# The router's products of a four-layer kernel turned round: weights still, tokens streaming

## The reference

```python
x = x + _L0_ffn_ref(_layernorm(x, axis=-1), expert_sel, keys, values, route_scale)

def _L0_ffn_ref(x, expert_sel, keys, values, route_scale):
    sel_logits = jnp.einsum('btd,ed->bte', x, expert_sel)       # 16 experts, D = 256
    sel_probs = jax.nn.sigmoid(sel_logits)
    _, sel_index = jax.lax.top_k(sel_probs, 4)
    sel_val = jnp.take_along_axis(sel_probs, sel_index, axis=-1)
    sel_val = sel_val / jnp.clip(sel_val.sum(-1, keepdims=True), 1e-09) * route_scale
    ...
```

## Time and profile before

| | |
|---|---|
| median of 3 runs | 1512.51 us (1511.04 to 1518.49) |
| the profiled execution | 1518.33 us |
| its span, first to last instruction | 1516.5 us |
| mean granted TensorE clock | 0.906 |
| PE busy | 1309.8 us, 86% |
| PE weight loads busy | 800.3 us, 53% |
| DVE busy | 935.9 us, 62% |
| ACT busy | 455.5 us, 30% |
| POOL busy | 325.8 us, 21% |

### The profile page before, as it was taken

The page is one execution under the profiler, slowest core; times in us unless marked ns, Lnnn a source line. Parts: engine busy times, 40 slices in busy tenths (PEclk is TensorE's granted clock), DMA queues, the critical chain, the costliest instruction groups (busy, mean ns, idle before and its releaser), DMA issues. The chain is left out here.

```text
span 1516.5 us, 17699 instructions
## 1 busy us (share of the span) xinstructions
PE 1309.8 (86%) x5358; PEld 800.3 (53%) x5358; DVE 935.9 (62%) x3450; ACT 455.5 (30%) x821; POOL 325.8 (21%) x600
## 2 busy tenths in 40 slices
PE   2676968999999899989989999999797606999997
PEld 2354645556465455646546564564354504766674
DVE  6657788677777567767766776677975282121110
ACT  2433441142224215222431530422322333223211
POOL 3211220023012203301220320221203203333222
PEclk9967978999999799889999999999998757999999
DMA  9002001200300300030030003012000151344321
GB/s 286 8 1 71 17 1 28 43 18 15 85 17 1 99 1 17 15 85 17 1 99 17 1 24 76 16 23 64 0 1 1 58 202 44 88 119 129 84 25 18
DMA packets 44857, 72.56 MB, mean 48 GB/s; under 512 B 8085, under 2 KB 26648, under 8 KB 44634
## 3 DMA queue, kind: packets, MB, share of 16 engines
q1 hardware_dynamic: 38618, 62.90, 14.2%
q0 software_dynamic: 6144, 8.52, 3.2%
HBM read 58.31 MB, written 13.11 MB: 47 GB/s over the span
## 5 line engine op out<-in xcount | busy, mean ns | idle before, releaser
L714 POOL TENSOR_SCALAR ve<-mv 128x2 f32<-128x2 f32 x74 | 16.8, 227 | 607.8 <-DVE mv L972 607.7
L1484 PE MATMUL ps<-x,keys 128*128 128x512 f32 x256 | 133.0, 646 | 0.4 <-DVE hT L1064 0.4
L1638 PE MATMUL ps<-hT,values 128*128 128x512 f32 x256 | 118.6, 592 | 0.0
L2099 PE MATMUL experts_ps<-experts_yT,experts_fc 128*128 128x512 f32 x256 | 114.2, 605 | 1.3 <-ACT experts_yT L2022 1.3
L2111 PE MATMUL experts_ps<-experts_fc,experts_hT 128*128 128x256 f32 x512 | 112.1, 380 | 0.8 <-ACT experts_hT L2034 0.8
L1484 PE MATMUL ps<-zT_second,w 128*128 128x512 f32 x224 | 103.3, 602 | 7.0 <-ACT big L1446 6.3
L2111 PEld LDWEIGHTS experts_ps<-experts_fc,experts_hT 128*128 128x128 f32 x512 | 96.6, 190 | 14.7 <-ACT experts_hT L2034 1.6
L1484 PE MATMUL ps<-w,big 128*128 128x256 f32 x448 | 101.1, 385 | 1.6 <-ACT big L1446 1.6
L1997 DVE SCALAR_TENSOR_TENSOR experts_o<-experts_ps,experts_wh,experts_b2w 128x256 f32<-128x256 f32 x32 | 15.5, 484 | 140.2 <-PE experts_ps L2111 140.2
L1484 PEld LDWEIGHTS ps<-w,big 128*128 128x128 f32 x448 | 85.6, 193 | 15.4 <-ACT big L1446 4.0
L2034 ACT ACTIVATE experts_hT<-experts_ps,experts_b 128x512 f32<-128x512 f32 x64 | 44.0, 687 | 158.0 <-PE experts_ps L2099 158.0
(11 more groups left out here) (436 smaller groups left out, 2520.1 us busy)
## 6 DMA issues: line engine op xcount, KB each, us to landing
gT<-expert_gates SPq DMA_DIRECT2D x16, 1024.0 KB, 10.2
experts_fc<-in_fc1T SPq DMA_DIRECT2D x8, 1024.0 KB
experts_fc<-in_fc2T SPq DMA_DIRECT2D x8, 1024.0 KB
xT<-in_xT SPq DMA_DIRECT2D x8, 512.0 KB, 3.7
x<-in_x SPq DMA_DIRECT2D x8, 512.0 KB, 3.5
expert_table<-tb SPq DMA_DIRECT2D x7, 528.0 KB, 10.3
out_x<-x SPq DMA_DIRECT2D x7, 512.0 KB, 9.6
w<-in_W SPq DMA_DIRECT2D x2, 1024.0 KB, 8.4
```

The costliest lines, as they stand in the source:

```text
L714: nc.gpsimd.tensor_scalar(o, i, c, None, ALU.add).then_inc(*tick(*event))
L1484: last = nc.tensor.matmul(o, l, r_, start=start, stop=stop)
L1638: last = nc.tensor.matmul(bank("O2", k), S["values"][:, c, k * P:(k + 1) * P], hT[:, c % RING, :], start=(c == 0), stop=(c == HC - 1))
L2099: last = nc.tensor.matmul(g_bank(m), fc1[e % 3][:, k, m * P:(m + 1) * P], yT[e % 2][:, k, :], start=(k == 0), stop=(k == DC - 1))
```

## The change

The products are turned round. In `route` the 17 columns of `sel` stand still and the 512 tokens of `xp` stream past, for both `k`; the logits come out with experts on the partitions, in partitions 64 to 80 of bank LG. The one column of 1/256 stands still while `sq` streams past, into partition 96. A new step, `turn_route`, follows `route` in all three tables: ACT copies 33 partitions by 512 of LG to `lists`, and PE turns them back in four pieces of 33 by 128 into bank LT, from which DVE goes on as before, with 33 columns for each group of tokens instead of 18 (mean in column 16, mean of squares in 32). `lists` grows to 128 partitions.

```diff
-    (ATTEND, 0, "attend_out"), (ATTEND, 0, "route"), (MID, 0, "mlp", 0), (ATTEND, 0, "attend_sum"), (KERN, 0, "powers", 2),
+    (ATTEND, 0, "attend_out"), (ATTEND, 0, "route"), (ATTEND, 0, "turn_route"), (MID, 0, "mlp", 0), (ATTEND, 0, "attend_sum"), (KERN, 0, "powers", 2),
...
-    first += [(("OT", k), k) for k in range(DC)] + [(("LG",), 2), (("GT",), 3)]
+    first += [(("OT", k), k) for k in range(DC)] + [(("LG",), 2), (("LT",), 3), (("GT",), 2)]
...
-        lists = sb("lists", [32 + E0, T])
+        lists = sb("lists", [P, T])
         g16 = lists[32:32 + E0, :]
+        route_rows = slice(64, 64 + 33)
...
-                    lg = bank("LG")[:, 0:NT * (E0 + 2)].rearrange("p (t e) -> p t e", t=NT)
-                    v.wait_ge(*at(b, "filled", "LG"))
-                    nc.vector.tensor_copy(ms[:], lg[:, :, E0:E0 + 2]).then_inc(*tick("ms"))
+                    lg = bank("LT")[:, 0:NT * 33].rearrange("p (t e) -> p t e", t=NT)
+                    v.wait_ge(*at(b, "filled", "LT"))
+                    nc.vector.tensor_copy(ms[:], lg[:, :, E0:2 * E0 + 1:E0]).then_inc(*tick("ms"))
...
+            def turn_route(b):
+                evacuate(b, lists[route_rows, :], bank("LG")[route_rows, :], "LG")
...
                 pe.wait_ge(*at(b, "emptied", "OT", DC - 1))
-                parts = [p for t in range(NT) for p in contract(o[:, t * (E0 + 2):t * (E0 + 2) + E0 + 1], [
-                    (xp[:, k, t * P:(t + 1) * P], S["sel"][:, k, :]) for k in range(DC)])]
                 pe.wait_ge(*open_(b, "LG"))
-                for o_, l, r_, start, stop in parts:
-                    nc.tensor.matmul(o_, l, r_, start=start, stop=stop)
+                for k in range(DC):
+                    nc.tensor.matmul(o[64:64 + E0 + 1, :], S["sel"][:, k, :], xp[:, k, :], start=(k == 0), stop=(k == DC - 1))
                 pe.wait_ge(*at(b, "sq", DC - 1))
+                for k in range(DC):
+                    last = nc.tensor.matmul(o[96:97, :], S["sel"][:, k, E0:E0 + 1], sq[:, k, :], start=(k == 0), stop=(k == DC - 1))
+                last.then_inc(*tick("filled", "LG"))
+
+            def turn_route(b):
+                pe.wait_ge(*at(b, "emptied", "LG"))
+                pe.wait_ge(*open_(b, "LT"))
                 for t in range(NT):
-                    for k in range(DC):
-                        last = nc.tensor.matmul(o[:, t * (E0 + 2) + E0 + 1:(t + 1) * (E0 + 2)], sq[:, k, t * P:(t + 1) * P],
-                                                S["sel"][:, k, E0:E0 + 1], start=(k == 0), stop=(k == DC - 1))
-                last.then_inc(*tick("filled", "LG"))
+                    last = nc.tensor.transpose(bank("LT")[:, t * 33:(t + 1) * 33], lists[route_rows, t * P:(t + 1) * P], ident[route_rows, route_rows])
+                last.then_inc(*tick("filled", "LT"))
```

More of the change, by code:

```diff
@@ L144 @@
     (MID, 0, "pick", 3, 3), (MID, 0, "picked", 0), (ATTEND, 1, "attend_out"), (ATTEND, 1, "attend_sum"), (KERN, 0, "kernel", 3),
-    (MID, 0, "text", 2), (ATTEND, 1, "route"), (MID, 0, "picked", 1), (ATTEND, 1, "gates", 0), (KERN, 0, "kernel", 4),
+    (MID, 0, "text", 2), (ATTEND, 1, "route"), (ATTEND, 1, "turn_route"), (MID, 0, "picked", 1), (ATTEND, 1, "gates", 0), (KERN, 0, "kernel", 4),
     (ATTEND, 1, "gates", 1), (ATTEND, 1, "gates", 2), (ATTEND, 1, "gates", 3), (KERN, 0, "kernel", 5), (ATTEND, 1, "spread"),
@@ L164 @@
     (LAST, "norm_out", 0), (LAST, "ffn_out", 1), (LAST, "ffn_add", 1), (LAST, "norm_out", 1), (ATTEND, "attend_sum"), (MID, "pick", 3, 1),
-    (ATTEND, "attend_out"), (MID, "pick", 3, 2), (ATTEND, "route"), (LAST, "scores", 0), (LAST, "scores", 1), (ATTEND, "gates", 0),
+    (ATTEND, "attend_out"), (MID, "pick", 3, 2), (ATTEND, "route"), (ATTEND, "turn_route"), (LAST, "scores", 0), (LAST, "scores", 1), (ATTEND, "gates", 0),
     (ATTEND, "gates", 1), (ATTEND, "gates", 2), (ATTEND, "gates", 3), (MID, "picked", 0), (LAST, "shift_scores"), (MID, "text", 2),
@@ L206 @@
     (ATTEND, 7, "attend_out"), (MID, 6, "stats_rows", 1), (MID, 6, "pick", 2, 1), (LAST, 5, "gelu", 5), (MID, 6, "pick", 2, 2),
-    (LAST, 5, "gelu", 6), (ATTEND, 7, "route"), (ATTEND, 7, "attend_sum"), (ATTEND, 7, "gates", 0), (LAST, 5, "gelu", 7),
+    (LAST, 5, "gelu", 6), (ATTEND, 7, "route"), (ATTEND, 7, "turn_route"), (ATTEND, 7, "attend_sum"), (ATTEND, 7, "gates", 0), (LAST, 5, "gelu", 7),
     (MID, 6, "pick", 2, 3), (ATTEND, 7, "gates", 1), (MID, 6, "weigh"), (LAST, 5, "ffn_out", 0), (MID, 6, "pick", 3, 0),
@@ L1020, in gates @@
                 if part == 1:
-                    lg = bank("LG")[:, 0:NT * (E0 + 2)].rearrange("p (t e) -> p t e", t=NT)
+                    lg = bank("LT")[:, 0:NT * 33].rearrange("p (t e) -> p t e", t=NT)
                     v.wait_ge(*at(b, "rr"))
                     nc.vector.tensor_tensor(sg[:, :, 0:E0], lg[:, :, 0:E0], rr[:].to_broadcast([P, NT, E0]),
-                                            ALU.mult).then_inc(*tick("emptied", "LG"))
+                                            ALU.mult).then_inc(*tick("emptied", "LT"))
                 if part == 2:
@@ L1473, in _ @@
             trips(a, {"steps": steps, "phases": phases, "powers": powers, "means": means, "bias": bias, "centre": centre, "kernel": kernel_taps,
-                      "keys": keys, "attend": attend, "attend_out": attend_out, "gates": gates, "spread": spread, "rows": rows, "text": text,
+                      "keys": keys, "attend": attend, "attend_out": attend_out, "gates": gates, "turn_route": turn_route, "spread": spread, "rows": rows, "text": text,
                       "weigh": weigh, "film": film, "transform": transform, "back": back, "hold": hold, "norm_ffn": norm_ffn,
@@ L1748, in table @@
                 transposes(b, "ST", uses=w.uses, parts=[(place(w, "ST")[0:E1, t * P:(t + 1) * P], w.sct[:, t, :]) for t in range(NT)])
-            trips(pe, {"powers": powers, "bias": bias, "centre": centre, "kernel": kernel_taps, "keys": keys, "attend": attend, "attend_out": attend_out, "route": route, "spread": spread, "mlp": mlp,
+            trips(pe, {"powers": powers, "bias": bias, "centre": centre, "kernel": kernel_taps, "keys": keys, "attend": attend, "attend_out": attend_out, "route": route, "turn_route": turn_route, "spread": spread, "mlp": mlp,
                        "rows": rows, "text": text, "text_scores": text_scores, "film": film, "transform": transform,
```

4 lines of the change are left out of this document (2 added, 2 removed).

## The result

| | before | after |
|---|---|---|
| median, runs side by side | 1514.99 us, 4 runs (1511.04 to 1518.49) | 1500.68 us, 4 runs (1494.98 to 1503.45) |
| ratio, 95% interval | | 0.9896 [0.9863, 0.993] |
| profiled execution, span | 1518.33, 1516.5 us | 1503.45, 1501.7 us |
| mean granted clock | 0.906 | 0.919 |

The change makes the kernel faster by 1.0%, outside the forecast range of 1505 to 1524 on its lower side. Run again, unchanged, on another chip, it had a median of 1503.26 of 12 runs, ratio 0.994 [0.9895, 0.9986]; all runs shown with the experiments together give 1516.7 for before (78 runs, 1495.7 to 1525.4) and 1501.7 for after (16 runs, 1489.3 to 1509.2).

A forecast was written before the change was run, and what follows sets the result against it. PE was busiest, but batches 2 to 5 were taken to hang on when routing products are ready for DVE. Batch terms, +3.6 (batch 0) to -1.9 (batch 7), summed to +1.0 us on 1512.51: 1513.5, range 1505 to 1524.

The forecast's parts named there:

- the overlap of the two kinds of products: In the route, `sq` beside the last `xp` products: none counted; by the skill page 0.43 us a batch, 3.4 in all.
- batches 3 and 4: DVE starts earlier after the route: -0.8 us in 3; -1.8 in 4, where PE's 3.04 us wait for `amT` also goes.
- The price of the new form: Route at full clock: eight passes, ACT's copy and four turns; DVE starts at 4.87 us, 1.10 later than batch 5 before.
- rival B: Longer idling ahead of `sct` spreads batch 3's long half-clock stretch to batches 2, 4 and 5: 1526.7 us; chance 0.20.
- Batch 0: ACT's copy stands ahead of the exponentials' table load, delaying the load and DVE 3.64 us: +3.6 us, bounds 1.1 and 3.9.
- Batch 1: PE's next products feed a DVE copy that PE waits for, all behind the route: +1.1 us.
- batch 2: DVE starts at 4.87 us after the route's start instead of 5.19: -0.3 us.
- batch 5: The route was already at full clock, so the new form makes PE and DVE later: +1.1 us.
- Batch 6: DVE is busy with statistics until `route_ms` at 5.17 us, later than 4.87: 0 us, bounds -1 and 0.5.
- Batch 7: PE sets the pace: +1.1 us for the route, but the half-clock stretch goes: -1.9 in all, bounds -3 and +1.1.
- D: PE was the bound after all; batches 2, 3, 4, 6 and 7 each win 3.4 us: 1506.8 us; chance 0.18.
- C: The clock falls anyway, only later, behind idle time and turns after the route: 1517.4 us; chance 0.15.

The follow-up runs named there:

- same_group: The changed kernel with the `sq` output put to partition 64 of bank LT, the `xp` output's partition group, and a second ACT copy; 1515.47 us, ratio to before 1.0032.
- serial: The changed kernel with PE made to wait until its `xp` products have landed before starting those on `sq`; 1509.57 us, ratio to before 0.9976.
- second trace of before: The kernel before the change, unaltered, run and traced once more; one time, 1507.77 us.
- gap_before: The kernel before, narrow products kept, with one 512-column product of constants in PE's idle gap ahead of the route, batches 2 to 6; 1504.68 us, ratio 0.9954.
- filler_before: The kernel before with two 512-column products of constants on PE ahead of its wait for `sct` in batches 2 to 5; 1506.42 us, ratio 0.9976.
- swap6: The changed kernel with ACT, in batch 6, copying the second half of the turned `x3` before the gates' exponential; 1491.49 us, ratio to before 0.9854.
- old_both: The kernel before with one product of constants ahead of the route (batches 2 to 6) and two ahead of the `sct` wait (2 to 5); 1492.32 us, ratio 0.9874.

## Why the prediction was wrong

Two steps failed: the overlap of the two kinds of products was put at nothing, and the terms of batches 3 and 4, -0.8 and -1.8, left the stretches at half clock behind `sct` as they were.

**The price of the new form** was right but for the overlap. Without it `route_ms` comes at 4.97, or 4.75 less the 0.22 of the added wait (4.87 forecast), PE idles 0.67 (0.66), the copy of 33x512 takes 0.58 (0.575), and the four turns take 0.36 from the first to PE's next work (0.43). The overlap was counted as nothing, and read from the Trainium skill as one hidden pass a batch, 3.4 us. It hid two and a half passes in batches 2 to 5, where the `sq` products wait for ACT's second square: the last pass ends 2.53 us after the first start, against 3.61 in `same_group`, 1.08 less. It hid all four possible in batches 1 and 7 (`route_ms` after 3.06), where the passes begin in pairs and the eight take 4 x 0.43 = 1.72 us from the first start. Timeline of PE, batch 1:

```profile
249.85 0.60 PE L1612 MATMUL ps<-x,sel 128*17 128x512 f32 x1
249.86 0.59 PE L1615 MATMUL ps<-e_buf,sel 128*1 128x512 f32 x1
```

5.8 to 8.3 us of the routed stretch came of the overlap. `serial`, which is the change without it, has 1509.57, inside the range. Part of that nearness is luck: its -6.8 and -6.9 in batches 3 and 4 against before, which were not forecast either, stand against +5.6 in batch 2. The Trainium skill, page "TensorE: Matmul & The Clock Gate", Part 3 on packing small matmuls, was right about the partition groups, and `same_group` agrees with it: 0.43 between passes in one group, 0.21 in two. But one hidden pass a batch was too few: each group keeps its own pace of 0.43, so the second runs beside the first from where its operand is ready.

**Batches 3 and 4** are the other step, and it failed in size. The terms were -0.8 and -1.8, with "What PE gains besides is idle time in front of `sct`"; measured, -7.8 and -7.4, and `serial`, without the overlap, has -6.8 and -6.9. By the second trace of before it is -1.4 and -7.4, and batch 5 has the other -7.0: about 7 us in each of two batches, whichever two they are. By the timelines of before and after, batch 3, the 7.8 are 1.9 us from the route to `sct`'s turning (16.2 to 14.3), 4.3 from there to the filter's first product (16.2 to 11.9) and 1.6 up to the next route. The earlier start was foreseen. That most of the half clock behind `sct`, 13.6 us in batch 3, would go too was not: it was taken as given, and rival B had it spread. `gap_before` and `filler_before` show with the old form what these stretches had cost: 13.6 and 12.0 us of the routed stretch. The idle time ahead of `sct` did grow, to 3.06 or nearly in four batches, as B had it, and still no long stretch followed in after. Why the long stretches went is open: `serial` shows one that came with the same 3.06 us.

**Batch 0**: +3.3 (+3.6 forecast), for the reason given; the wait of DVE grew from 1.60 to 4.15, not to about 5. That the number fits is partly luck: the overlap shortened this route too, and without it, in `serial`, the interval is 4.4 longer. **Batch 1**: +0.4 (+1.1), **batch 2**: +0.7 (-0.3), **batch 5**: +0.5 (+1.1). The two traces of before differ by more than these (122.8 and 124.0, 126.8 and 125.3, 125.6 and 133.1), so they confirm no term. **Batch 4's** wait for `amT`, 3.04, shrank as forecast, to 0.46:

```profile
645.33 1.98 PE L1488 MATMUL ps<-vf,amT 65*128 65x512 f32 x4 [0.46 <-ACT amT L1323]
```

**Batch 6**: +3.5 (0 forecast). It was right that `route_ms` does not move (5.16 against 5.17) and wrong that nothing else would. PE went past the route sooner and stood before ACT's late copy, and the clock did the rest. That place in ACT's queue was not looked at; `swap6` took back 4.0. **Batch 7**: from the route to the second half of `ffn_out` 13.2 us, not 16.6 in before: -3.4 (-1.9), of which 3.0 is the half-clock stretch that went as forecast. The second trace of before had no such stretch there and 13.7 us, so against it the change gains 0.5.

**The rivals.** D, that PE was the bound after all, gave 1506.8 and was the nearest, yet its reason is only half of it: `gap_before` shows that removing stretches at half clock gains time, while the idle time before `sct` shows that PE is not the bound throughout. C, a clock that falls behind the turns, did not happen: in batches 2 to 5 `wfilm` behind the turns took 3.65 us. The Trainium skill, same page, Part 4 on PE-mode transpose, has the full clock not come on for transposes; the trace of after doesn't bear out that this costs anything here, since a clock already full outlasted twelve turns in a row; in `gap_before`, with eight turns behind narrow products, it did fall (`wfilm` 5.34). B did not happen in after either; in `serial`, the route as it was priced, one batch of four went as B has it, with 13.6 us at half clock.

## What to carry to other kernels

Where two small products have fewer than 33 output rows each, give them different partition groups of 32 and let the second be ready early: here eight passes took the time of four where the second was ready at once, and of five and a half where it waited 0.66 us. Before widening or rewriting products that run at half clock, try one product of constants in the idle time just ahead of them; it took one product in each of five batches and gave nearly as much as turning the products round (1504.68 against 1503.26 on one chip). And when an engine gets faster, follow the queue of every engine that it will next wait for, step by step: the losses of 3.3 and 3.5 us were both a matter of two entries' order in ACT's queue.

## What was not expected of the hardware

- Passes of two output groups do not keep to the program's order: the first `sq` pass starts at 752.51, ahead of the third `xp` pass at 752.72, though all `xp` products stand before it in the program. While only `xp` passes ran they were 0.43 apart, and then each group went at 0.43 for itself.
- With one product (two passes, 1.02 us) in an idle gap of 0.84 us the clock was 1.00 through the 32 narrow passes behind it in all of batches 2 to 5, where before had 0.62 to 0.70 in three of the four. Without it the clock fell in some routes behind the same gap and not in others, and once, in `old_both`, it fell with no gap at all.
- A copy by ACT out of PSUM took 0.58 us for 16 and 33 partitions by 512 alike, and for one partition too:

```profile
763.12 0.58 ACT L1371 COPY lists<-ps 32x512 f32<-32x512 f32 x1 [3.04 <-PE ps L1618]
763.71 0.58 ACT L1372 COPY lists<-ps 1x512 f32<-1x512 f32 x1
```

Those are the two copies of `same_group` in the timeline of ACT, batch 5.
